# A mixture-of-experts stage on one core: the order of VectorE's two products, and one transfer for three copies of the weights

## The chip, the cores and the metric

The kernel runs on one NeuronCore of a Trainium2 chip. The metric is the device time of one execution in microseconds (us), lower is better; times of several executions are told by their median. The engines are called as in the profile: PE is TensorE's matmul, PEld its weight load, DVE is VectorE, ACT is ScalarE, POOL is GpSimd, SP (or SPq) is the queue that issues the DMAs.

## The reference

Two gated layers work on x, two batches of 512 tokens with 256 features. Layer 0 is an attention over a context and a feed-forward with weights of plus and minus one; layer 1 is an attention with 16 heads and a mixture of experts. Only the last part is touched:

```python
tidx, tw = _route(x, gate_w, gate_bias)        # 4 of 16 experts for each token, out of 2 of 4 groups
combine = jnp.zeros((n, E), x.dtype).at[jnp.arange(n)[:, None], tidx].add(tw)
g = jnp.einsum('nh,eih->nei', x, w1)
u = jnp.einsum('nh,eih->nei', x, w3)
hact = jax.nn.silu(g) * u * combine[:, :, None]
y = jnp.einsum('nei,ehi->nh', hact, w2)
shared = jnp.einsum('ni,hi->nh', jax.nn.silu(x @ ws1.T) * (x @ ws3.T), ws2)
```

There are 16 experts with 192 inner features each and one shared expert. Every expert is computed for every token, and the combination weight, zero for most tokens, does the routing.

## The kernel before

Every engine has its program written out by hand, and semaphores are the only order between engines. An engine works strictly through its own list: a wait at the head holds all that stands behind it.

The inner features of all experts are laid side by side (shared expert first, padded to 256) and cut into 26 tiles of 128. A tile is worked off in two jobs, one for each half (h = 0, 1) of the 1,024 tokens, so there are 52 jobs, j = 0 to 51. Each matrix is held as a rounded part and a rest ("hi" and "lo"), and a product takes three matmuls. The stages of a job:

- `gate_up(j)` on PE: 12 matmuls of 512 columns (line 270, by the helper `group`): first u into PSUM bank 2h+1, then g into bank 2h. It waits until job j-2 no longer needs these banks (`first(pe, "e_full", j - 1)`).
- silu on ACT (L1188): g from PSUM into `silu`.
- two products on DVE, in `job`: L1578 multiplies u (PSUM) by the combination weights (`comb`, SBUF) into `hcomb`; L1581 multiplies `hcomb` by `silu` into `hful` and counts `e_full`.
- hi on ACT (L1191): rounds `hful` into `eh[.., 0, ..]`. lo on DVE (L1586, `job_low`): the rest, `hful - hi`, counted by `e_lo`.
- `down(j)` on PE: 12 matmuls of 256 columns (L936), after `e_lo`. It adds the job's share of y up in PSUM banks 4 to 7.

In the steady loop PE's list is gate_up(j+2), down(j), gate_up(j+3), down(j+1) and so on. ACT's list is silu(j), hi(j), silu(j+1), hi(j+1). DVE's list is both products of j, lo(j), both products of j+1. POOL splits the weights of the next tiles into hi and lo (L555 to L564) out of staging buffers that SP refills.

The routing runs on DVE between the first jobs. ACT makes the sigmoid (L1197), then DVE's chain of small steps (L1608 to L1664) with job 1, job 2 and job 3 put in between at fixed places: the products of job 1 after L1619, lo(1) after L1635, the products of job 2 after L1648, lo(2) after L1652, and then the rest of the routing. Jobs 0 to 3 belong to the shared expert, whose weight is one, so they don't need the result; `comb` is set to ones by POOL for them. PE turns the result into rows of 16 experts (L959, banks 0 and 1), DVE copies them into `comb_rows` (L1669, two copies of 16x512), and SP writes them to a buffer in HBM (L366), each row three times, since an expert's 192 features are three halves of a tile. SP then loads the weights of a tile, broadcast over 64 partitions a half (L371, `comb_load`), for job 4 and on. These loads wait for `e_full` of the tile that used the buffer before.

```python
        sp.wait_ge(s["rt_copied"], 2)
        routed = comb_d.rearrange("(e r) n -> e r n", r=3)
        for r in range(3):
            for w in range(2):
                sp.dma_start(routed[:, r, 512 * w:512 * w + 512], comb_rows[w]).then_inc(s["comb_out"], 16)
        sp.wait_ge(s["comb_out"], 96)
```

PE's list over the start of the stage is: gate_up(0), the turning of the last normalised tokens (L575), down(0), the router's matmuls with 16 columns (L270), gate_up(1), gate_up(2), down(1), gate_up(3), down(2), the turning of the combination weights (L959), down(3), gate_up(4), gate_up(5), and then the loop from gate_up(6). Its end is gate_up(51), down(49), down(50), down(51). After that DVE adds y into x (L1486) and SP stores it (L387).

Of the kernel before, what the change touches and what calls it, by code (L numbers as in the profile page):

```python
# [15 lines left out]
F32 = mybir.dt.float32  # L16
# [3 lines left out]
ACT = mybir.ActivationFunctionType  # L20
# [3 lines left out]
NB, S, D = 2, 512, 256  # L24
# [14 lines left out]
E, EI = 16, 192  # L39
ET = 26  # L40
# [43 lines left out]
def build(nc, x_d, ctx_d, ctxT_d, mask_d, cst_d, bo_d, gbias_d, w0_d, k0_d, k1_d, k2_d, w1_d, gw_d, we_d,  # L84
          eye_d, ones_d, iota_d, out_d, comb_d):
    with ExitStack() as stack:
        program(nc, stack, x_d, ctx_d, ctxT_d, mask_d, cst_d, bo_d, gbias_d, w0_d, k0_d, k1_d, k2_d, w1_d,
                gw_d, we_d, eye_d, ones_d, iota_d, out_d, comb_d)


def program(nc, stack, x_d, ctx_d, ctxT_d, mask_d, cst_d, bo_d, gbias_d, w0_d, k0_d, k1_d, k2_d, w1_d,
            gw_d, we_d, eye_d, ones_d, iota_d, out_d, comb_d):
    def sb(name, shape, dt=F32):
        return stack.enter_context(nc.sbuf_tensor(name, shape, dt))

    def sem(name):
        return stack.enter_context(nc.semaphore(name))
# [45 lines left out]
    PS = stack.enter_context(nc.psum_tensor("PS", [P, 8, 512], F32))  # L143
# [45 lines left out]
    def key_block(i):  # L189

        return (i, slice(0, 512)) if i < 2 else ((i - 2) // 3, slice((i - 2) % 3 * 512, (i - 2) % 3 * 512 + 512))

    def key_low(eng, i, h):
# [22 lines left out]
    eh = R[:, 18432:20480].rearrange("p (r j n) -> p r j n", r=2, j=2)  # L216
    gw = [R[:, 9856 + 32 * j:9888 + 32 * j].rearrange("p (k n) -> p k n", k=KT) for j in range(2)]
    est = wst[:, 0:1536].rearrange("p (r n) -> p r n", r=2)
    silu = FA[:, 0:1024].rearrange("p (r n) -> p r n", r=2)
    hcomb = FA[:, 1024:2048].rearrange("p (r n) -> p r n", r=2)  # L220
    hful = FA[:, 2560:3584].rearrange("p (r n) -> p r n", r=2)
    comb = FB[:, 0:2048].rearrange("p (r n) -> p r n", r=2)
    gst = wst[:, 1536:1568]
    RT = FB[:, 2048:2816]
    comb_rows = [xs[0:E, :], FA[0:E, 3584:4096]]


    names = (
# [4 lines left out]
        "scored_context scored maxed expd turned p_hi p_lo pv_done o_tmp o_sum rsum rspread rbc at_norm at_hi at_lo wo_done x_att "  # L233
        "q_twice k_lo cx_twice pj_done pj_hi pj_lo w1q_split w1o_split xc_lo "
        "fw0_ready fw1_ready f1_done f2_done f_act f_hi f_lo f3_done x_ffn "
        "ones_set gw_split gate_done gate_sig rt_comb rt_turned rt_copied e_split_in e_split_out g_done u_done e_comb e_silu e_full e_hi e_lo e_y "
        "out_ready qlo_zeroed xc_zeroed dve_step pool_step pool_free").split()
    s = {n: sem(n) for n in names}

    def first(eng, name, value):  # L240

        if not isinstance(value, int) or value > 0:
            eng.wait_ge(s[name], value)
# [51 lines left out]
    def _(sp):  # L295
# [65 lines left out]

        sp.wait_ge(s["rt_copied"], 2)
        routed = comb_d.rearrange("(e r) n -> e r n", r=3)
        for r in range(3):
            for w in range(2):
                sp.dma_start(routed[:, r, 512 * w:512 * w + 512], comb_rows[w]).then_inc(s["comb_out"], 16)  # L366
        sp.wait_ge(s["comb_out"], 96)

        def comb_load(row, r, name):
            for half in range(2):  # L370
# [198 lines left out]
    def _(pe):  # L569
# [130 lines left out]
        for b in range(NB):  # L700
# [15 lines left out]
            for i in range(8):  # L716
# [4 lines left out]
                else:  # L721
                    p, n = (i - 2) // 3, (i - 2) % 3
# [22 lines left out]
            for i in range(8):  # L745
# [3 lines left out]
                for tt in range(TT):  # L749
                    c = 1792 + 512 * (i % 2) + tt * P  # L750
# [23 lines left out]
        for j in range(2 * MT):  # L774
            h, m = j // MT, j % MT
# [140 lines left out]
        def gate_up(j, tile, r, h):  # L916

            if h == 0:
                pe.wait_ge(s["e_split_in"], tile + 1)
            first(pe, "e_full", j - 1)  # L920
            for part in (1, 0):
                c = part * 256
                pairs = [((ew[r][0][:, c + kt * P:c + kt * P + P], ew[r][1][:, c + kt * P:c + kt * P + P]),
                          (LNH[:, kt, h * 512:h * 512 + 512], LNL[:, kt, h * 512:h * 512 + 512]))
                         for kt in range(KT)]
                group(PS[:, 2 * h + part, :], three(pairs)).then_inc(s["g_done" if part == 0 else "u_done"], 1)

# [21 lines left out]
        zero_banks(7)  # L949
        pe.wait_ge(s["gate_sig"], 1)  # L950
        gate_up(1, 0, 0, 1)
        gate_up(2, 1, 1, 0)
        down(1, 0, 0, 1)
        gate_up(3, 1, 1, 1)
        down(2, 1, 1, 0)
        pe.wait_ge(s["e_full"], 3)
        pe.wait_ge(s["rt_comb"], 1)
        for t in range(NB * TT):
            last = nc.tensor.transpose(PS[0:E, t // TT, (t % TT) * P:(t % TT) * P + P], wst[:, 1600 + t * E:1600 + t * E + E],  # L959
# [18 lines left out]
    def _(act):  # L978
        a_ = nc.scalar.activation
        col = {n: cst[:, i:i + 1] for i, n in enumerate(CONST)}  # L980

        def ln_root(n, cols=TT):
            act.wait_ge(s["ln_var"], n)
            a_(rstd[:, 8:8 + cols], rstd[:, 0:cols], ACT.Sqrt).then_inc(s["ln_std"], 1)

        def ln_split(n, b, dst, banks=None):

            act.wait_ge(s["ln_turned"], n)
            for kt in range(KT):
                a_(dst[:, kt, b * S:b * S + S], PS[:, (banks or LN_BANKS[b])[kt], :], ACT.Copy).then_inc(s["ln_hi"], 1)  # L990
# [77 lines left out]
        for b in range(NB):  # L1068
# [83 lines left out]
        def heads(g_, more):  # L1152
            for b in range(NB):
                C = 2 * g_ + b + 2
                nxt = b == 0 or more
                J1 = 28 * g_ + 14 * (b + 1)

                def next_projections(u):
                    project_hi(C + 1, J1, {UNITS: range(2), UNITS + 1: range(2, 4)}.get(u, ()))

                def next_norm(u):
                    if u == 2:
                        ln_root(4 * NB + 1)

                attention(L1, b, C, next_projections if nxt else next_norm)
                if nxt:
                    project_hi(C + 1, J1, range(4, 10))
                    exp(L1, C + 1, 0)
                else:
                    ln_split(3 * NB + 1, 0, LNH)  # L1170
                out_hi(L1, b, C)
                if nxt:
                    project_hi(C + 1, J1, range(10, 14))
# [9 lines left out]
        with act.Fori(0, NG1 - 1) as g_:  # L1183
            heads(g_, True)
        heads(NG1 - 1, False)
        def job(j, c):
            act.wait_ge(s["g_done"], AHEAD_G + j + 1)
            a_(silu[:, c % 2, :], PS[:, 2 * (c % 2), :], ACT.Silu).then_inc(s["e_silu"], 1)  # L1188
            act.wait_ge(s["e_full"], j + 1)
            act.wait_ge(s["e_y"], AHEAD_Y + j - 1)  # L1190
            a_(eh[:, c % 2, 0, :], hful[:, c % 2, :], ACT.Copy).then_inc(s["e_hi"], 1)  # L1191

        ln_root(4 * NB + 2)
        job(0, 0)
        ln_split(3 * NB + 2, 1, LNH)
        act.wait_ge(s["gate_done"], 2)
        a_(wst[:, 1728:1856], PS[:, 3, 0:P], ACT.Sigmoid).then_inc(s["gate_sig"], 1)  # L1197
        for c in range(1, 4):
            job(c, c)
        with act.Fori(1, ET // 2) as i:  # L1200
            for c in range(4):
                job(4 * i + c, c)


    @block.vector
    def _(dve):
        step = Steps(dve, "dve_step")
        v = nc.vector

        def inc(ins, name):  # L1210
            ins.then_inc(s[name], 1)
# [262 lines left out]
        for j in range(2 * MT):  # L1474
            h, m = j // MT, j % MT
# [97 lines left out]
        def job(j, c, comb_seen):  # L1573
            r, h = c // 2, c % 2
            dve.wait_ge(s["u_done"], j + 1)
            if comb_seen is not None:
                dve.wait_ge(s[f"comb_in{r}"], comb_seen)
            inc(v.tensor_tensor(hcomb[:, h, :], PS[:, 2 * h + 1, :], comb[:, r, h * 512:h * 512 + 512], ALU.mult), "e_comb")  # L1578
            dve.wait_ge(s["e_comb"], j + 1)
            dve.wait_ge(s["e_silu"], j + 1)  # L1580
            inc(v.tensor_tensor(hful[:, h, :], hcomb[:, h, :], silu[:, h, :], ALU.mult), "e_full")  # L1581

        def job_low(j, c):
            h = c % 2
            dve.wait_ge(s["e_hi"], j + 1)
            inc(v.tensor_tensor(eh[:, h, 1, :], hful[:, h, :], eh[:, h, 0, :].bitcast(F32), ALU.subtract), "e_lo")  # L1586

        dve.wait_ge(s["x_att"], 4 + 4 * NG1)
        dve.wait_ge(s["ln_turned"], 3 * NB + 1)
# [75 lines left out]
                            RT[:, 552:560].unsqueeze(2).to_broadcast([P, NT, E]), ALU.mult), "rt_comb")  # L1665
        job(3, 3, None)
        dve.wait_ge(s["rt_turned"], 1)
        for w in range(2):
            inc(v.tensor_copy(comb_rows[w], PS[0:E, w, :]), "rt_copied")  # L1669
        job_low(3, 3)  # L1670

        with dve.Fori(1, ET // 2) as i:
# [79 lines left out]
```

## Time and profile before

| | |
|---|---|
| median of 3 runs | 1258.67 us (1255.44, 1258.67, 1260.61) |
| profiled execution, its own time | 1258.23 us |
| its span in the profile | 1256.4 us |
| PE busy | 1096.7 us, 87% |
| PEld busy | 954.4 us, 76% |
| DVE busy | 898.7 us, 72% |
| ACT busy | 680.0 us, 54% |
| POOL busy | 279.0 us, 22% |
| mean granted clock of PE | 0.964 |

The span is the stretch between the first and the last event of the profile; the execution's own time is 1.83 us longer. Busy shares are averages over stages that have different limits, so the expert stage has to be read by itself. It takes the last 250 us, about a fifth of the span. An idle stretch of an engine costs only where another engine, or the end, waits for what comes behind it.

### The profile page before, as it was taken

The numbers are of one execution on the slowest core, as the hardware profiler recorded it, in microseconds if no ns is written. First come the engines' busy times: TensorE is split into PE (matmuls) and PEld (weight loads), VectorE is DVE, ScalarE is ACT, GpSimd is POOL, SyncE is SP. The second block draws the span as 40 slices with busy tenths as digits, with TensorE's granted clock in tenths as the row PEclk, the third lists the DMA queues.
The fourth block names the chain that finished last, engine by engine and source line by source line (L and its number), as shares of the span: only waits on it lengthen the run. The fifth ranks groups of instructions, "written<-read, shape, count | busy, mean of one in ns | idle before, by whom it ended". The sixth has DMA issues, their size and how long they took to land. (4 is left out here: it accounts for less than half of the span.)

```text
span 1256.4 us, 20142 instructions
## 1 busy us (share of the span) xinstructions
PE 1096.7 (87%) x6824; PEld 954.4 (76%) x6824; DVE 898.7 (72%) x1517; ACT 680.0 (54%) x1237; POOL 279.0 (22%) x280
## 2 busy tenths in 40 slices
PE   1869986996599789898989989899998988999998
PEld 1758876886488568787878878788887876888887
DVE  6689848998733677786878777887878755555555
ACT  3567755773211467675766767676867622222222
POOL 5050005003511310303030110403020023344432
PEclk9889998999799989999999999999999979999999
DMA  4000000003101000001000010000000003344332
GB/s 149 1 5 1 1 1 1 1 1 111 28 16 39 1 1 1 2 1 37 2 1 1 2 36 2 1 1 14 14 1 1 1 26 100 99 117 117 106 100 78
DMA packets 18045, 38.18 MB, mean 30 GB/s; under 512 B 3776, under 2 KB 10048, under 8 KB 17440
## 3 DMA queue, kind: packets, MB, share of 16 engines
q1 hardware_dynamic: 17952, 37.01, 10.1%
q8 instruction: 50, 0.82, 0.3%
q14 instruction: 43, 0.35, 0.1%
HBM read 35.76 MB, written 1.25 MB: 29 GB/s over the span
## 5 line engine op out<-in xcount | busy, mean ns | idle before, releaser
L270 PE MATMUL PS<-R 128*128 128x512 f32 (+2 forms) x2728 | 642.4, 380 | 60.1 <-DVE R L1337 14.2
L270 PEld LDWEIGHTS PS<-R 128*128 128x128 f32 x2728 | 461.2, 198 | 137.7 <-issue 32.8
L1291 DVE TENSOR_TENSOR R<-PS,R 128x512 fp32r<-128x512 f32 x352 | 225.4, 685 | 62.7 <-ACT R L1024 57.4
L1024 ACT ACTIVATE R<-PS 128x512 fp32r<-128x512 f32 x352 | 190.0, 596 | 147.2 <-PE PS L610 147.2
L610 PE MATMUL PS<-eye,FA 128*128 128x128 f32 x1408 | 189.2, 280 | 41.0 <-ACT FA L1000 31.6
L610 PEld LDWEIGHTS PS<-eye,FA 128*128 128x128 f32 x1408 | 155.5, 142 | 75.1 <-issue 26.0
L621 PEld LDWEIGHTS PS<-R 128*128 128x128 f32 x1408 | 186.1, 189 | 26.5 <-issue 11.8
L621 PE MATMUL PS<-R 128*128 128x256 f32 x1408 | 193.4, 283 | 8.7 <-DVE FB L1299 8.4
L1000 ACT ACTIVATE FA<-PS,nmax 128x1024 f32<-128x1024 f32 (+1 forms) x160 | 193.1, 1207 | 3.8 <-DVE nmax L1280 3.7
L1280 DVE TENSOR_REDUCE nmax<-PS 128x1 f32<-128x1024 f32 x128 | 155.4, 1214 | 5.8 <-issue 4.7
L424 POOL TENSOR_SCALAR R<-R 64x512 fp32r<-64x512 f32 x40 | 26.1, 654 | 437.9 <-ACT R L1141 378.0
L936 PEld LDWEIGHTS PS<-R 128*128 128x128 f32 x624 | 83.2, 195 | 11.7 <-DVE R L1586 5.5
L936 PE MATMUL PS<-R 128*128 128x256 f32 x624 | 85.5, 288 | 6.6 <-DVE R L1586 6.6
L1188 ACT ACTIVATE FA<-PS 128x512 f32<-128x512 f32 x52 | 31.1, 599 | 100.5 <-PE PS L270 100.5
L1581 DVE TENSOR_TENSOR FA<-FA 128x512 f32<-128x512 f32 x52 | 40.6, 780 | 49.8 <-ACT FA L1188 49.6
L1586 DVE TENSOR_TENSOR R<-FA,R 128x512 fp32r<-128x512 f32 x52 | 47.2, 908 | 37.0 <-ACT R L1191 36.9
L1191 ACT ACTIVATE R<-FA 128x512 fp32r<-128x512 f32 x52 | 32.9, 632 | 62.8 <-DVE FA L1581 42.1
L1470 DVE CAST R<-FA 128x512 fp32r<-128x512 f32 x32 | 21.0, 657 | 52.9 <-ACT FA L1131 52.9
L1299 DVE TENSOR_TENSOR FB<-PS,FA 64x256 f32<-64x256 f32 x80 | 34.2, 427 | 24.9 <-ACT FA L1011 22.7
L1011 ACT ACTIVATE FA<-PS 64x256 f32<-64x256 f32 x80 | 30.2, 377 | 35.0 <-PE PS L621 28.8
L1270 DVE CUSTOM_DVE_ANT_0 PS<-PS,FB 128x1024 f32<-128x1024 f32 x32 | 39.4, 1231 | 9.8 <-PE PS L270 9.7
L1131 ACT ACTIVATE FA<-PS,tg 128x512 f32<-128x512 f32 x16 | 11.0, 687 | 64.9 <-PE PS L270 64.9
(159 smaller groups left out, 1037.0 us busy)
## 6 DMA issues: line engine op xcount, KB each, us to landing
FB<-comb SPq DMA_DIRECT2D x48, 256.0 KB, 3.8
wst<-we_in SPq DMA_DIRECT2D x26, 384.0 KB, 4.0
wst<-w_in SPq DMA_DIRECT2D x4, 1024.0 KB, 5.7
wst<-w_in SPq DMA_DIRECT2D x3, 512.0 KB, 6.5
x<-x_in SPq DMA_DIRECT2D x2, 512.0 KB, 5.7
FB<-ctxT_in SPq DMA_DIRECT2D x2, 512.0 KB, 4.1
FB<-k_in SPq DMA_DIRECT2D x8, 128.0 KB, 2.5
FB<-ctxT_in SPq DMA_DIRECT2D x4, 256.0 KB, 4.0
```

The costliest lines, as they stand in the source:

```text
L270: last = mm(out, a, b, start=(n == 0), stop=(n == len(passes) - 1), skip_group_check=skip)
L610: last = nc.tensor.transpose(out[:, i * P:i * P + P], L.probs[:, u % 2, c:c + P], eye_ap)
L621: last = mm(PS[:, 7, 0:256], L.v[:, kt, hd, :], L.pt[j][:, k % 2, kt, :], start=(kt == 0 and j == 0), stop=(kt == L.kt - 1 and j == 1))
L936: last = mm(PS[:, 4 + T // 2, (T % 2) * D:(T % 2) * D + D], a, w, start=False, stop=False, skip_group_check=True)
L1000: a_(L.probs[:, u % 2, :], L.score[u % 2], ACT.Exp, bias=nmax[:, u % 2:u % 2 + 1], scale=1.0, accum_out=sums[:, u:u + 1]).then_inc(s["expd ...
L1024: a_(L.pt[0][:, (u // 2) % 2, 4 * g_:4 * g_ + 4, (u % 2) * P:(u % 2) * P + P], L.turn(u, g_).rearrange("p (t n) -> p t n", t=4), ACT.Copy) ...
L1270: step(v.tensor_tensor_reduce(L.score[r][:, 0:NCTX], L.score[r][:, 0:NCTX], maskbias, 1.0, -BIG, ALU.add, ALU.max, accum_out=nmax[:, 2 + r ...
L1280: inc(v.tensor_reduce(nmax[:, r:r + 1], L.score[r], AX.X, ALU.max, negate=True), "maxed")
L1291: inc(v.tensor_tensor(lo, turned, hi.bitcast(F32), ALU.subtract), "p_lo")
L1299: inc(v.tensor_tensor(at32[rows, p, qh * 256:qh * 256 + 256], PS[DH:P, 7, 0:256], L.tmp[rows, k % 2, :], ALU.add), "o_sum")
L1581: inc(v.tensor_tensor(hful[:, h, :], hcomb[:, h, :], silu[:, h, :], ALU.mult), "e_full")
L1586: inc(v.tensor_tensor(eh[:, h, 1, :], hful[:, h, :], eh[:, h, 0, :].bitcast(F32), ALU.subtract), "e_lo")
```

## The change

The two products of `job` change places: silu first, combination weights second. The first product, `e_prod`, now waits for silu, and frees both PSUM banks of the job; PE's gate_up waits for it instead of `e_full`. The combination weights are waited for between the two. The second factor of job 1 and 3 (h = 1) stays in FA and that of h = 0 goes to `xs`, so that `comb_rows` becomes one region of 1,024 columns.

On ACT the silu of the next job is put ahead of the hi of this one, from job 2 on. ACT also takes one of the two copies of the turned weights. SP writes the three copies of the rows in one DMA, by a source that is broadcast over the three.

```diff
-    hcomb = FA[:, 1024:2048].rearrange("p (r n) -> p r n", r=2)
-    hful = FA[:, 2560:3584].rearrange("p (r n) -> p r n", r=2)
+    hprod = FA[:, 1024:2048].rearrange("p (r n) -> p r n", r=2)
+    hful = [xs[:, :], FA[:, 2560:3072]]
...
-    comb_rows = [xs[0:E, :], FA[0:E, 3584:4096]]
+    comb_rows = FA[0:E, 3072:4096]
...
-        for r in range(3):
-            for w in range(2):
-                sp.dma_start(routed[:, r, 512 * w:512 * w + 512], comb_rows[w]).then_inc(s["comb_out"], 16)
-        sp.wait_ge(s["comb_out"], 96)
+        sp.dma_start(routed, comb_rows.unsqueeze(1).to_broadcast([E, 3, NB * S])).then_inc(s["comb_out"], 16)
+        sp.wait_ge(s["comb_out"], 16)
...
-            first(pe, "e_full", j - 1)
+            first(pe, "e_prod", j - 1)
...
-        pe.wait_ge(s["e_full"], 3)
+        pe.wait_ge(s["e_prod"], 3)
...
-        def job(j, c):
+        def job_silu(j, c):
             act.wait_ge(s["g_done"], AHEAD_G + j + 1)
+            first(act, "e_prod", j - 1)
             a_(silu[:, c % 2, :], PS[:, 2 * (c % 2), :], ACT.Silu).then_inc(s["e_silu"], 1)
+
+        def job_hi(j, c):
             act.wait_ge(s["e_full"], j + 1)
             act.wait_ge(s["e_y"], AHEAD_Y + j - 1)
-            a_(eh[:, c % 2, 0, :], hful[:, c % 2, :], ACT.Copy).then_inc(s["e_hi"], 1)
+            a_(eh[:, c % 2, 0, :], hful[c % 2], ACT.Copy).then_inc(s["e_hi"], 1)
...
+        job_silu(1, 1)
         for c in range(1, 4):
-            job(c, c)
-        with act.Fori(1, ET // 2) as i:
+            if c < 3:
+                job_silu(c + 1, c + 1)
+            else:
+                act.wait_ge(s["rt_turned"], 1)
+                a_(comb_rows[:, S:2 * S], PS[0:E, 1, :], ACT.Copy).then_inc(s["rt_copied"], 1)
+            job_hi(c, c)
+        job_silu(4, 0)
+        with act.Fori(1, ET // 2 - 1) as i:
             for c in range(4):
-                job(4 * i + c, c)
+                job_silu(4 * i + c + 1, (c + 1) % 4)
+                job_hi(4 * i + c, c)
+        for c in range(4):
+            if c < 3:
+                job_silu(2 * ET - 4 + c + 1, c + 1)
+            job_hi(2 * ET - 4 + c, c)
...
             dve.wait_ge(s["u_done"], j + 1)
+            dve.wait_ge(s["e_silu"], j + 1)
+            inc(v.tensor_tensor(hprod[:, h, :], PS[:, 2 * h + 1, :], silu[:, h, :], ALU.mult), "e_prod")
+            dve.wait_ge(s["e_prod"], j + 1)
             if comb_seen is not None:
                 dve.wait_ge(s[f"comb_in{r}"], comb_seen)
-            inc(v.tensor_tensor(hcomb[:, h, :], PS[:, 2 * h + 1, :], comb[:, r, h * 512:h * 512 + 512], ALU.mult), "e_comb")
-            dve.wait_ge(s["e_comb"], j + 1)
-            dve.wait_ge(s["e_silu"], j + 1)
-            inc(v.tensor_tensor(hful[:, h, :], hcomb[:, h, :], silu[:, h, :], ALU.mult), "e_full")
+            inc(v.tensor_tensor(hful[h], hprod[:, h, :], comb[:, r, h * 512:h * 512 + 512], ALU.mult), "e_full")
...
-        for w in range(2):
-            inc(v.tensor_copy(comb_rows[w], PS[0:E, w, :]), "rt_copied")
+        inc(v.tensor_copy(comb_rows[:, 0:S], PS[0:E, 0, :]), "rt_copied")
         job_low(3, 3)
```

How ACT's list moves over jobs 1 to 4, from the first silu after the sigmoid. Before (L1188 is silu, L1191 is hi):

```order
L1188 ACTIVATE FA<-PS 128x512 [waits g_done]
L1191 ACTIVATE R<-FA 128x512 [waits e_y,e_full]
L1188 ACTIVATE FA<-PS 128x512 [waits g_done]
L1191 ACTIVATE R<-FA 128x512 [waits e_y,e_full]
L1188 ACTIVATE FA<-PS 128x512 [waits g_done]
L1191 ACTIVATE R<-FA 128x512 [waits e_y,e_full]
```

In the changed kernel (L1187 is silu, L1192 is hi, L1206 the copy of the turned weights):

```order
L1187 ACTIVATE FA<-PS 128x512 [waits g_done]
L1187 ACTIVATE FA<-PS 128x512 [waits e_prod,g_done]
L1192 ACTIVATE R<-FA 128x512 [waits e_y,e_full]
L1187 ACTIVATE FA<-PS 128x512 [waits e_prod,g_done]
L1192 ACTIVATE R<-xs 128x512 [waits e_y,e_full]
L1206 ACTIVATE FA<-PS 16x512 [waits rt_turned]
L1192 ACTIVATE R<-FA 128x512 [waits e_y,e_full]
L1187 ACTIVATE FA<-PS 128x512 [waits e_prod,g_done]
```

hi(1) now stands behind silu(2), hi(2) behind silu(3), and hi(3) behind the copy.

ACT's list at the end of the changed kernel, from silu(49) on, where before silu and hi of each job alternate:

```order
L1187 ACTIVATE FA<-PS 128x512 [waits e_prod,g_done]
L1192 ACTIVATE R<-xs 128x512 [waits e_y,e_full]
L1187 ACTIVATE FA<-PS 128x512 [waits e_prod,g_done]
L1192 ACTIVATE R<-FA 128x512 [waits e_y,e_full]
L1187 ACTIVATE FA<-PS 128x512 [waits e_prod,g_done]
L1192 ACTIVATE R<-xs 128x512 [waits e_y,e_full]
L1192 ACTIVATE R<-FA 128x512 [waits e_y,e_full]
```

The last four rows are hi(49), silu(51), hi(50) and hi(51).

DVE's list from job 3's second product to job 4's lo (between the two parts stands the loop's entry). Before:

```order
L1581 TENSOR_TENSOR FA<-FA 128x512 [waits e_silu,e_comb]
L1669 COPY xs<-PS 16x512 [waits rt_turned]
L1669 COPY FA<-PS 16x512
L1586 TENSOR_TENSOR R<-FA,R 128x512 [waits e_hi]
...
L1578 TENSOR_TENSOR FA<-PS,FB 128x512 [waits comb_in0]
L1581 TENSOR_TENSOR FA<-FA 128x512 [waits e_silu,e_comb]
L1586 TENSOR_TENSOR R<-FA,R 128x512 [waits e_hi]
```

In the changed kernel:

```order
L1595 TENSOR_TENSOR FA<-FA,FB 128x512 [waits e_prod]
L1682 COPY FA<-PS 16x512 [waits rt_turned]
L1600 TENSOR_TENSOR R<-FA,R 128x512 [waits e_hi]
...
L1591 TENSOR_TENSOR FA<-PS,FA 128x512 [waits e_silu,u_done]
...
L1595 TENSOR_TENSOR xs<-FA,FB 128x512 [waits comb_in0]
L1600 TENSOR_TENSOR R<-xs,R 128x512 [waits e_hi]
```

One copy is gone from this list, and the wait for the first broadcast weights (`comb_in0`) has moved from job 4's first product to its second. The places of lo(1) and lo(2) inside the routing chain are as before, and PE's list is the same in both kernels.

## Rows read from the trace of the kernel before

**Rows 1.** Page, busy time, share of span, instructions:
```profile
PE 1096.7 (87%) x6824; PEld 954.4 (76%) x6824; DVE 898.7 (72%) x1517; ACT 680.0 (54%) x1237; POOL 279.0 (22%) x280
```

**Rows 2.** Windows: length, busy us of PE, PEld, DVE, ACT, POOL, clock, DMA:
```profile
1100.00:1200.00 100.00, 100.00 (x577) 88.27 (x575) 55.87 (x73) 29.57 (x48) 41.28 (x49) 1.00 0.40 109
```

**Rows 3.** Timeline of the steady loop: start, length, engine, line, [idle before <-releaser]:
```profile
1085.07 2.91 PE L270 MATMUL PS<-R 128*128 128x512 f32 x12
1085.55 0.63 ACT L1191 ACTIVATE R<-FA 128x512 fp32r<-128x512 f32 x1 [1.11 <-DVE FA L1581]
1086.21 0.69 DVE L1586 TENSOR_TENSOR R<-FA,R 128x512 fp32r<-128x512 f32 x1 [0.78 <-ACT R L1191]
1086.82 0.68 DVE L1578 TENSOR_TENSOR FA<-PS,FB 128x512 f32<-128x512 f32 x1
1087.82 1.59 PE L936 MATMUL PS<-R 128*128 128x256 f32 x12
```

**Rows 4.** Timeline of PE over the stage's start:
```profile
1014.55 2.90 PE L936 MATMUL PS<-R 128*128 128x256 f32 x12 [1.65 <-DVE R L1586]
1023.22 7.28 PE L270 MATMUL PS<-R 128*128 128x512 f32 x24
1033.06 2.54 PE L936 MATMUL PS<-R 128*128 128x256 f32 x12 [2.56 <-DVE R L1586]
1035.40 3.67 PE L270 MATMUL PS<-R 128*128 128x512 f32 x12
1039.42 1.67 PE L936 MATMUL PS<-R 128*128 128x256 f32 x12 [0.35 <-DVE R L1586]
1042.85 1.03 PE L959 MATMUL PS<-eye,wst 128*16 128x128 f32 x8 [1.76 <-DVE wst L1664]
1045.87 1.87 PE L936 MATMUL PS<-R 128*128 128x256 f32 x12 [1.99 <-DVE R L1586]
1047.54 7.10 PE L270 MATMUL PS<-R 128*128 128x512 f32 x24
1055.70 3.02 PE L270 MATMUL PS<-R 128*128 128x512 f32 x12 [1.07 <-DVE FA L1581]
```

**Rows 5.** Timeline of DVE over the stage's start:
```profile
1028.51 0.69 DVE L1581 TENSOR_TENSOR FA<-FA 128x512 f32<-128x512 f32 x1 [1.73 <-ACT FA L1188]
...
1038.58 0.69 DVE L1586 TENSOR_TENSOR R<-FA,R 128x512 fp32r<-128x512 f32 x1
...
1043.94 0.67 DVE L1669 COPY xs<-PS 16x512 f32<-16x512 f32 x1
...
1045.14 0.67 DVE L1586 TENSOR_TENSOR R<-FA,R 128x512 fp32r<-128x512 f32 x1
1054.24 0.69 DVE L1578 TENSOR_TENSOR FA<-PS,FB 128x512 f32<-128x512 f32 x1 [8.42 <-DMA FB<-comb]
1054.96 0.69 DVE L1581 TENSOR_TENSOR FA<-FA 128x512 f32<-128x512 f32 x1
```

**Rows 6.** Timeline of ACT, job 3, and jobs 4 and 5:
```profile
1039.11 0.60 ACT L1188 ACTIVATE FA<-PS 128x512 f32<-128x512 f32 x1 [1.52 <-PE PS L270]
...
1055.76 0.63 ACT L1191 ACTIVATE R<-FA 128x512 fp32r<-128x512 f32 x1 [3.24 <-DVE FA L1581]
1056.30 0.58 ACT L1188 ACTIVATE FA<-PS 128x512 f32<-128x512 f32 x1
```

**Rows 7.** Timeline of SP: the last write and the first loads:
```profile
1047.49 0.42 SPq L366 DMA_DIRECT2D comb<-FA  x1
1049.17 2.40 SPq L371 DMA_DIRECT2D FB<-comb  x4
```

**Rows 8.** Timeline of job 51:
```profile
1246.86 0.60 ACT L1188 ACTIVATE FA<-PS 128x512 f32<-128x512 f32 x1 [2.06 <-PE PS L270]
1249.02 0.69 DVE L1586 TENSOR_TENSOR R<-FA,R 128x512 fp32r<-128x512 f32 x1 [0.77 <-ACT R L1191]
```

**Rows 9.** Windows, columns as in rows 2:
```profile
1048.00:1049.00 1.00, 1.00 (x4) 0.81 (x3) 0.00 (x0) 0.00 (x0) 0.92 (x2) 0.50 0.23 55
```

More of the change, by code:

```diff
@@ L235, in program @@
         "fw0_ready fw1_ready f1_done f2_done f_act f_hi f_lo f3_done x_ffn "
-        "ones_set gw_split gate_done gate_sig rt_comb rt_turned rt_copied e_split_in e_split_out g_done u_done e_comb e_silu e_full e_hi e_lo e_y "
+        "ones_set gw_split gate_done gate_sig rt_comb rt_turned rt_copied e_split_in e_split_out g_done u_done e_prod e_silu e_full e_hi e_lo e_y "
         "out_ready qlo_zeroed xc_zeroed dve_step pool_step pool_free").split()
@@ L1185, in _ @@
         heads(NG1 - 1, False)
-        def job(j, c):
+        def job_silu(j, c):
             act.wait_ge(s["g_done"], AHEAD_G + j + 1)
+            first(act, "e_prod", j - 1)
             a_(silu[:, c % 2, :], PS[:, 2 * (c % 2), :], ACT.Silu).then_inc(s["e_silu"], 1)
+        def job_hi(j, c):
             act.wait_ge(s["e_full"], j + 1)
             act.wait_ge(s["e_y"], AHEAD_Y + j - 1)
-            a_(eh[:, c % 2, 0, :], hful[:, c % 2, :], ACT.Copy).then_inc(s["e_hi"], 1)
+            a_(eh[:, c % 2, 0, :], hful[c % 2], ACT.Copy).then_inc(s["e_hi"], 1)
         ln_root(4 * NB + 2)
-        job(0, 0)
+        job_silu(0, 0)
+        job_hi(0, 0)
         ln_split(3 * NB + 2, 1, LNH)
@@ L1585, in job_low @@
             dve.wait_ge(s["e_hi"], j + 1)
-            inc(v.tensor_tensor(eh[:, h, 1, :], hful[:, h, :], eh[:, h, 0, :].bitcast(F32), ALU.subtract), "e_lo")
+            inc(v.tensor_tensor(eh[:, h, 1, :], hful[h], eh[:, h, 0, :].bitcast(F32), ALU.subtract), "e_lo")
         dve.wait_ge(s["x_att"], 4 + 4 * NG1)
```

## The prediction

> **What bounds the kernel now.** I read four views. The page's busy times say that PE leads with 87% [rows 1], but that is a mean over all stages; the change touches only the last fifth. So I took windows there: in 100 us of the steady expert loop PE is busy for 100.00 at full clock, DVE for 55.87 and ACT for 29.57 [rows 2]. In the timeline of the loop a job is 2.75 us of gate_up (from 1085.07 to 1087.82) and 1.43 us of down, 4.18 us together, with no gap [rows 3]. No edit of DVE or ACT can shorten this loop. It could only lengthen it.
>
> What is left is the start of the stage, until gate_up(6) begins at 1055.70, and the end. At the start PE stands idle at six places behind job 0's products, and each time the timeline names the releaser [rows 4]: 1.65, 2.56, 0.35 and 1.99 us before a down, each for DVE's lo; 1.76 us before the turning of the weights; 1.07 us before gate_up(6), for `hful` of job 4. The reader should see that the first five hang on DVE's routing chain and the lo steps put into it, and that only the last hangs on the transfer of the combination weights, since DVE waited 8.42 us for it [rows 5]. So the transfer holds PE up by 1.07 us and no more, though it takes far longer.
>
> **The loop.** Removed is nothing: DVE has two products of the same size before and after. What changes is the order in which they wait. Let G be the end of gate_up(j+1), when silu(j+1) starts. Now hi(j) comes behind it: ACT's step from one instruction to the next is 0.54 us (1055.76 to 1056.30, [rows 6]), hi takes 0.63, and lo starts about 0.04 behind it and takes 0.69 [rows 3], so lo(j) ends at about G+1.95. down(j) starts at G+4.18. Before, hi(j) came ahead of silu(j+1). The margin was about 5 us and is now 2.2 us. The first product of j+1 follows lo(j) by 0.61 (1086.21 to 1086.82, [rows 3]) and ends at G+2.6; gate_up(j+3), which waits for it, starts at G+5.6, a margin of 3.0. The weights' reload is asked for by the second product, some 2 us later than before, and is used three jobs (12.5 us) on, where the first loads took about 5 us from the issue at 1049.17 to 1054.24 [rows 5, 7]. All of this is hidden by PE, and I cost the loop at nothing. If the cover of 2.2 us were gone, each further 0.1 us would cost 46 times that.
>
> **The start, term by term.**
> - Job 0: the first product stood beside silu; now it follows it. Both products in a row are 0.72 apart (1054.24 and 1054.96, [rows 5]). PE waits for lo(0) [rows 4], so down(0), and the router and the sigmoid behind it, come **0.7 us** later.
> - Job 1: DVE waited 1.73 us for silu(1) before L1581 [rows 5]. Now the first product comes behind that wait too, and all the routing behind it is another **0.7 us** later. hi(1) behind silu(2) costs nothing: gate_up(2) ends at 1030.50 [rows 4], and lo(1) is wanted only when PE's 2.56 us are over.
> - Job 2 is the new wait. hi(2) must let silu(3) pass, and silu(3) needs gate_up(3), which ends at 1035.40 + 3.67 = 1039.07; it started at 1039.11 [rows 4, 6]. hi(2) then starts at 1039.65, ends at 1040.28, and lo(2) starts at 1040.32. In the profile lo(2) started at 1038.58 [rows 5]. Everything here is late by the same 1.4 us on both sides, so the difference stands: **1.7 us**, and behind lo(2) in DVE's list is the rest of the routing, for which PE's turning waits. So two engines pay for it, in a chain.
> - Job 3 and the copies: DVE drops the second copy (0.6 us), but hi(3) stands behind ACT's copy. From the start of the copies lo(3) began 1.20 us later (1043.94 to 1045.14, [rows 5]). Now it is 0.54 for the copy, 0.63 for hi and 0.04: 1.21. I take **0**. A 16x512 copy on ACT isn't in the trace; silu of 128x512 at 0.60 [rows 6] is nearest, and half or double of that would be -0.3 or +0.6.
> - The transfer: from the end of the second copy, about 1045.2, to the first load at 1049.17 [rows 7] is 4.0 us, with six issues. One issue and one landing: the last small write took 1.7 us from 1047.49 to 1049.17, so at the least 1.7; at the most 5, what the first pair of loads with 512 KB took. The new one has 192 KB, nearer the small one; I take 2.5. The loads then start 1.5 us earlier against the chain, but the chain is 3.1 late. It doesn't matter, for gate_up(6) now waits for the first product of job 4, which needs only silu(4). down(4) needs the weights, and the slack there is about 2 us. So the merged transfer brings **0** by itself, and PE's wait of 1.07 us before gate_up(6) goes: **-1.1 us**. Late next is lo(4), not by enough.
>
> The Trainium skill (DMA: Bandwidth & Descriptors, Rules for kernel authors) says to coalesce many small transfers into one large one, because below 64 KB one pays mostly overhead. The case's six writes of 32 KB are of this kind. By that rule 1.5 us would be gained, and the sum would be 2.9 instead of 4.4; the releasers in the rows speak against its reaching the end.
>
> **The clock.** Between 1035 and 1046 PE has gaps; gate_up(4) and (5) then take 7.10 us [rows 4] where two full-speed ones take 5.5 [rows 3]. That is 1.6 us for one fall to the lower level, and from 1048 to 1049 the granted clock was indeed 0.50, which is 1.2 GHz [rows 9]. With the new gaps (about 3.3 before down(1) and 2.0 before down(2)) PE has the same 2.7 us of small work in 8.5 us rather than in 6.8, so a fall may come before the turning of the weights, 1.03 us long at full clock [rows 4], which would then take twice that, on the chain. Bounds: -1.6 if the fall goes away, +1.0 for the turning, +1.6 for one more fall. I take **+0.5**, half of the turning.
>
> **The end.** Before, lo(51) started 2.16 us after silu(51) (1246.86 and 1249.02, [rows 8]), and down(51) behind it. Now ACT does silu(51), hi(50), and DVE does lo(50), both products of 51, and only then hi(51) and lo(51): 0.54 + 0.63 + 0.04 to lo(50), 0.61 to the product, 0.72 to the second, 0.69 + 0.10 + 0.63 + 0.04 to lo(51), 4.00 us. DVE's addition into x and all stores follow. That is **+1.8 us** with nothing to hide it.
>
> **The sum.** 0.7 + 0.7 + 1.7 + 0 + 0 - 1.1 + 0.5 + 1.8 = +4.3 us, on the profiled execution's own time of 1258.23: 1262.5 us. The median of the runs shown is 0.44 above that execution. About 0.5%, or 6.3 us, is what a measurement here can tell from no change, so the forecast is slower, but within that.
>
> **The rivals.**
> 1. *The clock takes more.* A fall before the turning (1.0) and a further one over gate_up(3) or gate_up(5) (1.6 each, two of them 3.2): 1258.23 + 3.8 + 4.2 = 1266.2 us. For it: PE's idle time around job 2 grows by about 2 us. Against: the profile has gaps of 1.76 and 1.99 us close together [rows 4], and one fall before gate_up(4) [rows 9] was all they brought. It decides as soon as two more stretches run at 1.2 GHz. The skill (TensorE: Matmul & The Clock Gate, The HAM clock gate) says that the clock halves after idling and returns after sustained work; the trace agrees that work after gaps runs at the lower level.
> 2. *The loop breaks.* If DVE and POOL hold each other up so that lo(j) misses down(j) by 0.3 us in each of 46 jobs, it is +14, 1276 us. lo has been seen up to about 1.2 us long; that is 0.5 of the 2.2 us of margin.
> 3. *The new wait at job 2 doesn't bite*, because DVE's chain is late there for another reason, so that its 1.7 falls away: +2.6, 1260.8 us. A gate_up(3) at full clock (2.75 instead of 3.67, [rows 3, 4]) would give back 0.9 of it.
> 4. *The transfer was the true bound* and PE closes its gaps with it: the wait of 1.07 and one clock fall of 1.6 go, and the end costs its 1.8. That is 1258.23 + 1.8 - 1.1 - 1.6 = 1257.3 us, no change. Against it stand four releasers that name lo. To be faster by over 0.5% it would need most of the 9 us of idle time, which nothing here removes.
>
> **How the numbers follow.** Forecast 0.58, rival 1 0.16, rival 2 0.04, rival 3 0.14, rival 4 0.08. The forecast's own spread of the copy, the transfer and the clock is about 2 us, and the three runs shown lie 5 us apart, which is why a median of them moves. Range 1258.3 to 1267.3: it takes in rivals 3 and 1. Beyond 6.3 us slower lie rivals 1 and 2, most of them, and a tenth of the forecast: 0.24. Faster by as much: 0.03, for an error of mine about the idle time. Within: 0.73.
>
> **What the profile of the changed kernel would show.** In the loop PE stays at 4.18 us a job, with hi starting some 0.5 us after silu. In the start, lo(2) is preceded by an idle DVE of about 1.7 us, released by ACT's hi; before down(2) PE is idle for about 2 us; gate_up(6) follows gate_up(5) without a gap; gate_up(6) starts about 2.5 us later than before. At the end lo(51) starts 4.0 us after silu(51). I am wrong if PE has gaps in the loop, if lo(2) starts without a wait, or if the transfer's landing is again what PE waits for.

## The result, and the profile after

The changed kernel takes 1263.81 us in the median of 19 runs, beside 1258.38 us for 19 runs of the kernel before. The ratio is 1.0048, with a 95% interval of 1.0037 to 1.0059, or 6.0 us slower (4.7 to 7.4). The ratio is that of the means; the medians are 5.4 us apart. The forecast was +4.3 us, the right direction and a little less than the interval holds. Two executions that took far longer than all others (5876 us of the kernel before, 1582 us of e6) are left out of the ratios below.

The busy times of the page, to be held against [rows 1], and the steady loop, against [rows 2]. A row of windows has the stretch, its length, the busy us of PE, PEld, DVE, ACT and POOL, PE's granted clock, and the DMA's share and GB/s.

```profile
PE 1102.3 (87%) x6824; PEld 958.3 (76%) x6824; DVE 889.7 (70%) x1516; ACT 675.1 (53%) x1238; POOL 280.6 (22%) x280
```
```profile
1100.00:1200.00 100.00, 100.00 (x576) 88.31 (x575) 51.06 (x73) 26.79 (x48) 42.92 (x48) 1.00 0.40 109
```

PE is full in the loop as before, and from the start of down(4) to that of down(49) both kernels take 188.10 us: nothing is lost there. PE's timeline over the start, against [rows 4]:

```profile
1009.19 2.89 PE L270 MATMUL PS<-R 128*128 128x512 f32 x12
...
1017.06 2.90 PE L934 MATMUL PS<-R 128*128 128x256 f32 x12 [2.36 <-DVE R L1600]
...
1025.73 7.36 PE L270 MATMUL PS<-R 128*128 128x512 f32 x24
1036.13 2.89 PE L934 MATMUL PS<-R 128*128 128x256 f32 x12 [3.04 <-DVE R L1600]
1038.81 3.29 PE L270 MATMUL PS<-R 128*128 128x512 f32 x12
1044.96 1.72 PE L934 MATMUL PS<-R 128*128 128x256 f32 x12 [2.86 <-DVE R L1600]
1047.53 1.86 PE L957 MATMUL PS<-eye,wst 128*16 128x128 f32 x8 [0.86 <-DVE wst L1678]
1051.32 2.93 PE L934 MATMUL PS<-R 128*128 128x256 f32 x12 [1.92 <-DVE R L1600]
1054.05 9.59 PE L270 MATMUL PS<-R 128*128 128x512 f32 x36
```

The gaps before down(0), down(1) and down(2) grew from 1.65, 2.56 and 0.35 to 2.36, 3.04 and 2.86. gate_up(4), (5) and (6) now run as one piece of 36 matmuls, without the wait of 1.07. The turning takes 1.86 instead of 1.03, down(3) 2.93 instead of 1.87. DVE and ACT around job 2, against [rows 5, 6], each from its own timeline:

```profile
1043.36 1.46 DVE L1600 TENSOR_TENSOR R<-xs,R 128x512 fp32r<-128x512 f32 x1 [1.58 <-ACT R L1192]
```
```profile
1042.14 0.60 ACT L1187 ACTIVATE FA<-PS 128x512 f32<-128x512 f32 x1 [7.90 <-PE PS L270]
1042.64 0.62 ACT L1192 ACTIVATE R<-xs 128x512 fp32r<-128x512 f32 x1
```

hi(2) (L1192) follows silu(3) (L1187), and DVE stands idle for 1.58 us ahead of lo(2), with the rest of the routing behind it. SP, against [rows 7], and the clock, against [rows 9] (windows, as in rows 2):

```profile
1050.14 0.71 SPq L364 DMA_DIRECT2D comb<-FA  x1
1053.86 2.52 SPq L369 DMA_DIRECT2D FB<-comb  x4
```
```profile
1048.00:1049.00 1.00, 1.00 (x7) 0.57 (x5) 0.69 (x1) 0.00 (x0) 0.00 (x0) 0.50 0.00 0
1052.00:1053.00 1.00, 1.00 (x7) 1.00 (x7) 0.00 (x0) 0.00 (x0) 0.00 (x0) 0.50 0.96 106
```

The merged write takes 3.72 us from its issue to the first load. The clock is at its lower level (0.50, 1.2 GHz) while the turning and down(3) run. The last job, against [rows 8]:

```profile
1251.78 0.60 ACT L1187 ACTIVATE FA<-PS 128x512 f32<-128x512 f32 x1 [3.06 <-PE PS L270]
1252.27 0.62 ACT L1192 ACTIVATE R<-xs 128x512 fp32r<-128x512 f32 x1
1252.92 0.69 DVE L1600 TENSOR_TENSOR R<-xs,R 128x512 fp32r<-128x512 f32 x1 [2.16 <-ACT R L1192]
1253.54 0.69 DVE L1591 TENSOR_TENSOR FA<-PS,FA 128x512 f32<-128x512 f32 x1
...
1255.64 0.69 DVE L1600 TENSOR_TENSOR R<-FA,R 128x512 fp32r<-128x512 f32 x1 [0.70 <-ACT R L1192]
```

lo(51) (the last row) starts 3.86 us after silu(51) (the first), where it was 2.16.

The two spans differ by 6.3 us (1256.4 and 1262.7). Of these, gate_up(0) began at 1007.28 and now at 1009.19, so 1.9 us lie ahead of the stage, where no line was changed; 3.0 lie between gate_up(0) and down(4) (51.28 us and 54.28); 1.7 at the last three downs; and what follows the start of down(51) is 0.3 shorter.

### The profile page after: what moved, and what is told of

It is laid out like the page before. It is cut to its first block and busy times, and to the rows that moved or that the text cites. A ratio compares the mean times of both kernels' runs of the same rounds, so it can differ in the third digit from the quotient of the medians.

```text
span 1262.7 us, 20176 instructions
## 1 busy us (share of the span) xinstructions
PE 1102.3 (87%) x6824; PEld 958.3 (76%) x6824; DVE 889.7 (70%) x1516; ACT 675.1 (53%) x1238; POOL 280.6 (22%) x280
## 5 line engine op out<-in xcount | busy, mean ns | idle before, releaser
L1187 ACT ACTIVATE FA<-PS 128x512 f32<-128x512 f32 x52 | 31.1, 599 | 162.4 <-PE PS L270 162.4
L1484 DVE CAST R<-FA 128x512 fp32r<-128x512 f32 x32 | 25.2, 786 | 53.7 <-ACT FA L1129 53.7
L1600 DVE TENSOR_TENSOR R<-xs,R 128x512 fp32r<-128x512 f32 x26 | 19.2, 739 | 51.7 <-ACT R L1192 51.7
L1600 DVE TENSOR_TENSOR R<-FA,R 128x512 fp32r<-128x512 f32 x26 | 18.0, 693 | 42.6 <-ACT R L1192 42.6
L406 POOL TENSOR_TENSOR R<-FA,R 64x512 fp32r<-64x512 f32 x32 | 41.0, 1282 | 16.0 <-ACT FA L1147 13.7
```

What stands on the lines that cost most here:

```text
L406: g.tensor_tensor(L1.k[other, 2 + h, cols], pair1_keys[n][rows, :], L1.k[rows, 2 + h, cols].bitcast(F32), ALU.subtract).then_inc(s["k_lo"], 1)
L1600: inc(v.tensor_tensor(eh[:, h, 1, :], hful[h], eh[:, h, 0, :].bitcast(F32), ALU.subtract), "e_lo")
```

## The experiments

Every run was compared with runs of the kernel before on the same chip. Ratios are to those, with their 95% intervals. "Start" is the time from gate_up(0) to down(4) in the one profile that each run has, "router" the part of it from down(0) to gate_up(1), "end" the time from down(49) to down(51), all in us between the starts of the first matmuls. The clock of a single profile moves these numbers by some us, as the three rows of the kernel before show, so a stage is told from one profile and a kernel's time from the ratio.

| kernel | ratio (95%) | start | router | end |
|---|---|---|---|---|
| before, first profile | 1 | 51.28 | 8.67 | 3.11 |
| c1, before again | 0.9995 (0.9975 to 1.0016) | 48.02 | 6.03 | 3.11 |
| c3, before a third time | 0.9990 (0.9968 to 1.0012) | 48.20 | 6.01 | 3.11 |
| changed, first profile | 1.0048 (1.0037 to 1.0059) | 54.28 | 8.67 | 4.81 |
| c2, changed again | 1.0045 (1.0026 to 1.0063) | 54.29 | 8.67 | 4.81 |
| e1, ACT's order back | 1.0035 (1.0016 to 1.0054) | 50.99 | 8.67 | 3.76 |
| e2, ACT's order back at the start | 1.0033 (1.0019 to 1.0048) | 50.98 | 8.67 | 4.81 |
| e3, six writes | 1.0061 (1.0041 to 1.0082) | 54.24 | 8.67 | 4.82 |
| e4, write twice | 1.0064 (1.0038 to 1.0091) | 55.79 | 8.67 | 4.81 |
| e5, before with one write | 0.9978 (0.9957 to 0.9999) | 46.97 | 4.66 | 3.11 |
| e7, e1 and job 0 back | 1.0003 (0.9987 to 1.0020) | 46.28 | 4.65 | 3.76 |
| e8, before with job 0 late | 1.0025 (1.0009 to 1.0041) | 51.76 | 8.67 | 3.11 |
| e6, parts kept | 0.9960 (0.9937 to 0.9983) | 48.07 | 8.67 | 3.11 |
| e9, parts kept again | 0.9939 (0.9920 to 0.9959) | 44.88 | 6.14 | 3.11 |

**ACT's order back.** e1 restores it everywhere, e2 at the start alone (the first part of this edit). The lines that go with it are left out.

```diff
...
-            if c < 3:
-                job_silu(c + 1, c + 1)
-            else:
+            job_silu(c, c)
+            if c == 3:
                 act.wait_ge(s["rt_turned"], 1)
...
-        job_silu(4, 0)
-        with act.Fori(1, ET // 2 - 1) as i:
+        with act.Fori(1, ET // 2) as i:
             for c in range(4):
-                job_silu(4 * i + c + 1, (c + 1) % 4)
+                job_silu(4 * i + c, c)
                 job_hi(4 * i + c, c)
...
```

> The changed kernel with ACT's old order in all jobs (silu(j), hi(j)); products, transfer and ACT's copy stay as changed. Theory A (the cost is hi standing behind the next silu, at job 2 and at the end): lo(2) starts without a wait on hi, lo(51) starts 2.9 us after silu(51) instead of 4.0, and 0.7 + 0.7 - 1.1 + 0.7 = +1.0 us is left against the kernel before, 1259.4. Theory B (the cost is the order of the two products, or what the loop pays for it): the time stays near +5, 1263.5.

> The changed kernel with ACT's old order in jobs 1 to 3 alone; the loop and the end keep the silu ahead. Theory A: the 1.7 us at job 2 go, and with them the slow turning and the slow down(3) where the clock fell (about 1.5), so 2 to 3 us less than the changed kernel, about 1261; the end still costs its 1.5. If the clock fall comes whatever job 2 does, only 1.7 go. Theory B: no change, 1263.8.

PE's timeline in e2, down(2), the turning and down(3):

```profile
1043.40 1.67 PE L934 MATMUL PS<-R 128*128 128x256 f32 x12 [0.52 <-DVE R L1598]
1046.69 1.03 PE L957 MATMUL PS<-eye,wst 128*16 128x128 f32 x8 [1.63 <-DVE wst L1676]
1049.65 2.15 PE L934 MATMUL PS<-R 128*128 128x256 f32 x12 [1.92 <-DVE R L1598]
```

The gap before down(2) falls from 2.86 to 0.52, the turning takes 1.03 again, and the start is 3.3 us shorter, where theory A had 2 to 3. The end goes from 4.81 to 3.76 in e1 and stays at 4.81 in e2; in e1 lo(51) starts 2.82 us after silu(51), as expected (2.9). So in the profiles hi behind the next silu cost 3.3 us at the start and 1.05 at the end. The router ran alike, 8.67 us, in all these profiles, so it has no part in that difference.

The ratios are coarser. They fell by 0.0013 in e1 and 0.0015 in e2, or 1.6 and 1.9 us, give or take 2.8 and 2.3. That holds the profile's 3.3 for e2, but the 4.4 for e1 (3.3 and 1.05) only at its edge, and it doesn't tell e1 from e2. Theory A had +1.0 us for e1, about 1.0008; 1.0016 to 1.0054 was measured. Its whole stage, from gate_up(0) to down(51), is only 0.4 us longer than in the first profile of before, but 2.5 longer than in the mean of that kernel's three profiles. What else of the change is left in e1 is taken up under the controls.

**The write undone, and doubled.**

```diff
-        sp.dma_start(routed, comb_rows.unsqueeze(1).to_broadcast([E, 3, NB * S])).then_inc(s["comb_out"], 16)
-        sp.wait_ge(s["comb_out"], 16)
+        for r in range(3):
+            for w in range(2):
+                sp.dma_start(routed[:, r, 512 * w:512 * w + 512], comb_rows[:, 512 * w:512 * w + 512]).then_inc(s["comb_out"], 16)
+        sp.wait_ge(s["comb_out"], 96)
```

> The changed kernel with the six writes of the kernel before in place of the merged one. Theory A (the transfer is hidden behind job 4's first product and gate_up(6)): no change, within 0.5 us; the stretch from the copies' end to the first load differs by 0.2 us. Rival (the merged write is worth what it saves in issues, 1.5 us): 1265.3.

> The changed kernel with the merged write done twice, one behind the other, so that the first load starts about 3.7 us later: the disputed cost doubled. Theory A: the cover behind job 4 was about 2 us, so about 1.5 to 2.5 us reach down(4), which then waits for lo(4), and the time rises by that, 1265.8. If the transfer lies on the path in full, +3.7; if the cover is larger than 3.7, 0.

SP's timeline in e3, and in e4:

```profile
1053.00 2.67 SPq L366 DMA_DIRECT2D comb<-FA  x6
1056.92 2.40 SPq L371 DMA_DIRECT2D FB<-comb  x4
```
```profile
1048.77 0.71 SPq L364 DMA_DIRECT2D comb<-FA  x1
1052.49 0.60 SPq L366 DMA_DIRECT2D comb<-FA  x1
1056.10 2.92 SPq L371 DMA_DIRECT2D FB<-comb  x4
```

Six writes take 3.92 us to the first load, one takes 3.72. The start of e3 is that of the changed kernel within 0.04 us: the transfer is hidden. The ratio can't decide this: 1.0061 with its interval holds the changed kernel's 1.0048 as well as the rival's 1.0060. It is the profile that speaks against the rival. In e4 the loads start 3.61 us later in the chain, DVE waits for them, and PE waits in turn before down(4):

```profile
1061.34 0.69 DVE L1597 TENSOR_TENSOR xs<-FA,FB 128x512 f32<-128x512 f32 x1 [3.12 <-DMA FB<-comb]
```
```profile
1063.64 1.66 PE L936 MATMUL PS<-R 128*128 128x256 f32 x12 [1.40 <-DVE R L1602]
```

The start grows by 1.51 us, so 2.1 of the 3.6 were covered, as theory A had it (a cover of about 2). The ratio, 1.0064, is 2 us above the changed kernel's, within an interval of 3 us to either side.

**The controls.** c1 and c3 are the kernel before, c2 is the changed one.

> The kernel before once more, unchanged, as a control. In the first profiles all kernels with the change had two places ahead of the expert stage (about 800 and 1002 us) where PE's clock stayed low 3.4 us longer than in the one profile of before, 2.9 us together. If that is chance of the clock, this profile may show it too and the ratio is 1.000; if it belongs to the change, this profile shows neither.

> The changed kernel once more, unchanged. If the two places are chance, the time ahead of the stage is within 2 us of before's on average, and the ratio is near the 1.0037 that the stage's own +4.5 us makes; if they belong to the change, the ratio is 1.005 or more again.

> The kernel before a third time. Ratio 1.000; under theory C the stretch from down(0) to gate_up(1) is shorter than 8.67 in some of its profiles (it was 8.67 and 6.03 in the first two).

gate_up(0) began at 1005.58 and 1010.11 us in c1 and c3 and at 1009.97 in c2; over all profiles of the table it lies between 1005.6 and 1014.4, and the latest is that of a fast kernel (e6). The time ahead of the stage thus differs as much between profiles of one kernel as between kernels, and the 1.9 us between the first two profiles say nothing of the change. With the router it is otherwise. Its 24 matmuls with 16 columns in c3, and in e8:

```profile
1017.15 2.90 PE L936 MATMUL PS<-R 128*128 128x256 f32 x12 [1.65 <-DVE R L1586]
1019.85 2.91 PE L270 MATMUL PS<-R 128*128 128x16 f32 x24
```
```profile
1017.91 2.90 PE L936 MATMUL PS<-R 128*128 128x256 f32 x12 [2.36 <-DVE R L1592]
1020.61 5.12 PE L270 MATMUL PS<-R 128*128 128x16 f32 x24
```

In the kernel before both speeds occur: 5.12 us in its first profile, 2.91 in c3.

**Job 0 alone.** e7 is e1 with job 0's combination weights first again, its semaphore counts moved to match; e8 is before with job 0 silu first. This is e8's edit:

```diff
             dve.wait_ge(s["u_done"], j + 1)
+            if isinstance(j, int) and j == 0:
+                dve.wait_ge(s["e_silu"], 1)
+                inc(v.tensor_tensor(hcomb[:, 0, :], PS[:, 1, :], silu[:, 0, :], ALU.mult), "e_comb")
+                dve.wait_ge(s["e_comb"], 1)
+                inc(v.tensor_tensor(hful[:, 0, :], hcomb[:, 0, :], comb[:, 0, 0:512], ALU.mult), "e_full")
+                return
```

> e1_act_order_back, and job 0 with the combination weights first again. In the profiles so far the router's 24 matmuls took 5.1 us at the lower clock in all six kernels in which lo(0) came 0.7 us later, but 2.7 to 5.1 in the others. Theory C (the 0.7 us longer gap before down(0) settles the clock low over the router and up to gate_up(1)): PE's gap before down(0) is 1.65 again, the stretch from down(0) to gate_up(1) is shorter than 8.67 in this or in part of the runs, and the ratio falls from e1's 1.0035 to about 1.001. Rival (the clock there is chance alike in all): only the 0.7 us go, ratio 1.003.

> The kernel before with job 0 alone silu first, so that lo(0) and down(0) come 0.7 us later and nothing else changes. Theory C: 0.7 us and a mean of some 2 us of clock, ratio 1.002 to 1.003, the stretch from down(0) to gate_up(1) 8.67. Rival (chance): 0.7 us, ratio 1.0005.

The router part is 8.67 us in all seven profiles whose lo(0) is late (gap of 2.4 before down(0)), and 4.65, 4.66, 6.01, 6.03, 6.14, 8.67 and 8.67 in the seven with the short gap of 1.6: 6.4 in the mean, 2.3 less. Were the gap without effect, such a split (nine slow ones, and all seven late ones among them) would come about once in a hundred times. The clock over it in e5, and in the changed kernel (windows):

```profile
1017.00:1021.00 4.00, 4.00 (x37) 4.00 (x36) 0.76 (x2) 1.11 (x2) 0.00 (x0) 1.00 0.02 4
```
```profile
1017.00:1024.00 7.00, 6.94 (x33) 6.97 (x33) 1.11 (x2) 1.45 (x2) 0.00 (x0) 0.50 0.01 2
```

e8 adds 0.7 us of work order to the kernel before and is 0.25% slower, 3.1 us; e7 takes the same away from e1 and lands at 1.0003. e8's interval excludes the rival's 1.0005. e7's excludes 1.003, nearly so when e1's own interval is counted in. Both agree with 0.7 us and about 2.3 of clock. That the later down(0) is what holds the clock low is thus shown in the mean; what decides it in one execution of the kernel before is not.

**The merged write in the kernel before.** The edit is that of the change for `hful`, `comb_rows` and the DMA alone.

> The kernel before with the merged write alone (the second factors and the rows move to the places of the changed kernel, nothing else). In before, PE's last wait of 1.07 us did hang on the weights' arrival. Theory A: the merged write saves only 0.2 us from the copies to the first load, so that wait becomes about 0.9, time unchanged. Rival (each issue saved is gained): the wait of 1.07 us goes, 1255.6.

PE's wait before gate_up(6):

```profile
1053.55 3.02 PE L270 MATMUL PS<-R 128*128 128x512 f32 x12 [0.78 <-DVE xs L1579]
```

It was 1.07 in the first profile of before, and it is 0.89 in e8, which has the six writes too. So 0.1 to 0.3 us are gained here, the 0.2 of the transfer and little else, and the rival's gain of the whole 1.07 is not there. The ratio, 0.9957 to 0.9999, just excludes theory A's unchanged time and holds the rival's 0.9991; it leaves room for more than either. The router ran at full clock in this profile, which the edit doesn't explain, and what the rest of the ratio is stays open.

**What is worth keeping.** e6 and e9 are one kernel, twice: ACT's order of before, jobs 0 to 3 with one product from PSUM, silu first for jobs 4 to 47, the combination weights first for the last four, the merged write. Of their edit, `job` alone:

```diff
+            if comb_seen is None:
+                dve.wait_ge(s["e_silu"], j + 1)
+                inc(v.tensor_tensor(hful[h], PS[:, 2 * h + 1, :], silu[:, h, :], ALU.mult), "e_full")
+                return
+            if not isinstance(j, int):
...
+                inc(v.tensor_tensor(hcomb[:, h, :], PS[:, 2 * h + 1, :], silu[:, h, :], ALU.mult), "e_prod")
...
+                inc(v.tensor_tensor(hful[h], hcomb[:, h, :], comb[:, r, h * 512:h * 512 + 512], ALU.mult), "e_full")
```

> Built from the kernel before: ACT's order of before; jobs 0 to 3 drop the multiplication by one (a single product from PSUM, so the ones of POOL go too; the result is the same); jobs 4 to 47 silu first, jobs 48 to 51 combination weights first as before; merged write; ACT's copy behind hi(3). Theory A: job 0 and 1 cost nothing, job 2 is 0.7 us shorter, job 3 with the copies 0.6 shorter, PE's 1.07 us wait for job 4 goes, the end as before: stage 2.4 us shorter than before, 1256. Theory B (silu-first products cost in the loop): PE has gaps in the loop and it is slower than before.

> e6_parts_kept once more, for its size: its first profile had the slow router and still a stage 3.2 us shorter than the first profile of before. Theory A: ratio 0.996 to 0.998 again.

PE's timeline in e9, down(1) to gate_up(6):

```profile
1033.05 1.87 PE L936 MATMUL PS<-R 128*128 128x256 f32 x12 [2.17 <-DVE R L1598]
1034.71 4.35 PE L270 MATMUL PS<-R 128*128 128x512 f32 x12
1038.90 1.59 PE L936 MATMUL PS<-R 128*128 128x256 f32 x12
1041.74 1.03 PE L959 MATMUL PS<-eye,wst 128*16 128x128 f32 x8 [1.25 <-DVE wst L1675]
1044.15 2.55 PE L936 MATMUL PS<-R 128*128 128x256 f32 x12 [1.37 <-DVE R L1598]
1046.49 9.07 PE L270 MATMUL PS<-R 128*128 128x512 f32 x36
```

Its start is 3.2 us shorter than that of before where the router is alike (48.07 against 51.28, and 44.88 against 48.02 and 48.20, about), and the end is the same. It beats both kernels, at ratios of 0.9960 and 0.9939 to the kernel before. 2.4 us were expected; 5.0 and 7.7 were measured, of which the profiles show 3.2. For e9 a ratio of 0.996 to 0.998 was expected, and its interval, 0.9920 to 0.9959, lies just below. The rest may be clock again, and is not settled; nor was it measured which of the parts brings how much.

## Why the prediction was right, and where it was off

Direction, mechanism and most terms were right. The table has the forecast terms beside what the stage shows, in us between starts of PE's groups: the changed kernel's first profile less the first of before, and less the mean of before's three (its stage from gate_up(0) to down(51) takes 247.20 us; before 242.48, and 240.37 in the mean).

| term | forecast | against the first profile | against the mean of three |
|---|---|---|---|
| job 0, gate_up(0) to down(0) | +0.7 | +0.60 | +0.76 |
| the router, down(0) to gate_up(1) | 0 | 0.00 | +1.77 |
| job 1, gate_up(1) to down(1) | +0.7 | +0.55 | +0.53 |
| job 2, down(1) to the turning | +1.7 | +1.62 | +1.62 |
| the copies, and the clock over the turning | 0 + 0.5 | +0.77 | +0.77 |
| PE's wait, down(3) to down(4) | -1.1 | -0.54 | -0.32 |
| the loop | 0 | 0.00 | 0.00 |
| the end | +1.8 | +1.71 | +1.71 |
| sum | +4.3 | +4.7 | +6.8 |

- **The loop at nothing:** right. PE is at 100.00 of 100 us, and silu-first costs nothing there.
- **Job 0, +0.7:** the wait grew from 1.65 to 2.36, as said. What was missed is that this step has a second price, the router's. The first profile of before happened to have the router at 1.2 GHz already, and I took that row as the kernel's habit; two more profiles of the same kernel show 6.0 instead of 8.67. All fourteen profiles, with e7 and e8 among them, put the price at some 2.3 us in the mean.
- **Job 1, +0.7:** down(1) came 10.39 us behind gate_up(1) instead of 9.84: 0.55.
- **Job 2, +1.7:** the mechanism is right, and DVE's wait of 1.58 is there. PE's gap before down(2) is 2.86, where about 2 was forecast. From down(1) to down(2) it is 8.83 instead of 6.36, 2.5 us, because lo(2) also took 1.46 instead of 0.69: it now runs beside POOL's split of the next weights (L555, from 1043.01 on for 1.26), which waits for the end of gate_up(3), as silu(3) ahead of hi(2) does. 0.86 came back before the turning, where another DVE step had been stretched in the same way before (L1658; 1.12 in the kernel before, 0.29 now). Net 1.6.
- **Copies, 0:** right. lo(3) starts 1.14 us after the start of the copies, 1.20 before.
- **The transfer, 0 by itself:** right, but for its size. It saves 0.2 us, not 1.5; the one large write takes 3.7 us from its issue to the first load, where the last of six small ones took 1.7, and 2.5 was assumed. The rule of the Trainium skill (DMA: Bandwidth & Descriptors, Rules for kernel authors), to coalesce, gives little in this case, 0.2 us, and e3's profile shows none of it reaching the end of the changed kernel. (By that rule the prediction's sum would have been 2.8 instead of 4.3; its 2.9 and 4.4 are slips.)
- **PE's wait before gate_up(6), -1.1:** the wait is gone, but this was no fixed cost of the kernel before. In c1 and c3, the same kernel, little of it is left: the last matmul of gate_up(5) and the first of gate_up(6) start 0.35 and 0.54 us apart, where 0.23 is usual and 1.46 stood in the first profile. Their down(3) ran at the lower clock, so PE was late itself; c3's rows:

```profile
1045.84 2.93 PE L936 MATMUL PS<-R 128*128 128x256 f32 x12 [1.99 <-DVE R L1586]
1048.57 9.89 PE L270 MATMUL PS<-R 128*128 128x512 f32 x36
```

  From down(3) to down(4) the three profiles of before take 12.69, 12.28 and 12.46 us and the changed kernel 12.15, so 0.3 is gained in the mean. In e1, e2 and e7, whose down(3) ran at 1.8 to 2.2 us, it is 11.3, which is the full gain; in the changed kernel, whose down(3) took 2.93, most of it is lost again.
- **The clock, +0.5:** this is the term that was mis-sized. The turning took 1.86 instead of 1.03, 0.83 longer (I took half of 1.03): it is 1.03 in all three profiles of before and wherever ACT's order was put back. The router adds 1.8 against the three profiles, 2.3 over all. That makes some 3 us where I had 0.5. The slow down(3) can't be charged to the change, since two of before's three profiles have it too. Rival 1, to which I had given 0.16, was right that more stretches would run at the lower clock, but put the second one over gate_up(3) or gate_up(5); it came at the router.
- **The end, +1.8:** 1.7.

The measured 6.0 us (4.7 to 7.4) agree with the mean's 6.8. That the forecast of +4.3 matches the first column so well is partly luck: the profile it was read from had a slow router, which hid one price of the change, and a wait that the kernel before shows in full in one profile of three.

## What to carry to other kernels

An instruction moved ahead on an in-order engine must be asked what it waits for: silu(3) waited for a gate_up, and so did everything that was put behind it, at the one place where there was no cover. A gain for the steady loop is worth nothing if PE is full there, and the same order can be kept out of the first and the last jobs. One profile is one draw of the clock: before a stretch at the lower level, or a short wait behind it, is taken as given, look at a second profile of the same kernel.

## What was not expected of the hardware

- 24 matmuls with 16 columns took 5.1 us at a granted clock of 0.50 or 2.7 at 1.00. With 2.4 us of idle PE before down(0) they ran at 0.50 in seven of seven profiles, with 1.6 in two of seven. In these nine PE was busy throughout, and the clock still rose only under the 512-column matmuls of gate_up(1) or (2); in c3 it was at 0.90 in the mean of the first us of the 16-column ones, and at 1.00 in the next.
- One write of 192 KB from 16 partitions took 3.7 us from issue to the next DMA, which waits for it, six writes of 32 KB took 3.9.
- Two DVE steps with both inputs in SBUF took 1.46 and 1.12 us instead of 0.69 and 0.29 when a POOL split ran beside them; moving a step moves such a meeting too.
